# Attention kernel on one core: key norms as two split-format matmul passes, squares split by GpSimd, query norms issued first

## The reference, cut to what matters

```python
q, k, v = (cproj(Wq), cproj(Wk), cproj(Wv))      # complex, 16 heads of 64
qr = q * phase[None]; kr = k * phase[None]       # rotary
E = jnp.exp(jnp.clip(-mu[:, None, None] * dt[None], MIN_EXP, 0.0))
s = jnp.einsum('bihd,bjhd->bhij', qr, jnp.conj(kr)).real
qn = (q.real ** 2 + q.imag ** 2).sum(-1).transpose(0, 2, 1)
kn = (k.real ** 2 + k.imag ** 2).sum(-1).transpose(0, 2, 1)
maha = jnp.maximum(qn[..., None] + (E * E)[None] * kn[:, :, None, :] - 2.0 * E[None] * s, 0.0) / V[None]
logits = coef * jnp.log1p(maha / nu[None, :, None, None]) - 0.5 * DH_ * jnp.log(V)[None]
A = jax.nn.softmax(jnp.where(causal[None, None], logits, -jnp.inf), axis=-1)
out = jnp.einsum('bhij,bjhd->bihd', A.astype(v.dtype), v)
```

## Time and profile before

| what | us |
|---|---|
| median of 3 runs | 2018.23 |
| lowest and highest | 2016.56, 2019.1 |
| the profiled execution's own time | 2022.78 |
| its span in the profile | 2021.0 |

### The profile page before, as it was taken

The page is one execution under the profiler, slowest core; times in us unless marked ns, Lnnn a source line. Parts: engine busy times, 40 slices in busy tenths (PEclk is TensorE's granted clock), DMA queues, the critical chain, the costliest instruction groups (busy, mean ns, idle before and its releaser), DMA issues. The chain is left out here.

```text
span 2021.0 us, 32368 instructions
## 1 busy us (share of the span) xinstructions
PE 1818.7 (90%) x9824; PEld 1374.4 (68%) x9824; DVE 1603.8 (79%) x3302; ACT 1422.5 (70%) x2739; POOL 867.4 (43%) x686
## 2 busy tenths in 40 slices
PE   3777999689999999999999999999999997499998
PEld 2444666458777777777777777777777776266665
DVE  5589776678987987888888798798798886667776
ACT  3422444568988988888899898888888987444443
POOL 0299001055655655565565565566456553000000
PEclk9886999789999999999999999999999998699999
DMA  4000002322222222222222222222222221000000
GB/s 144 6 0 1 0 0 70 110 66 53 68 71 48 66 64 57 66 58 62 66 59 64 50 69 69 48 66 67 54 66 53 66 53 32 2 6 6 10 10 11
DMA packets 46341, 97.94 MB, mean 48 GB/s; under 512 B 6320, under 2 KB 20272, under 8 KB 46160
## 3 DMA queue, kind: packets, MB, share of 16 engines
q1 hardware_dynamic: 46160, 95.75, 18.9%
HBM read 18.13 MB, written 10.49 MB: 14 GB/s over the span
## 5 line engine op out<-in xcount | busy, mean ns | idle before, releaser
L1036 POOL TENSOR_TENSOR rot<-by_cos,crossed 128x1024 f32<-128x1024 f32 x128 | 305.3, 2385 | 507.4 <-PE pS L851 287.5
L1044 POOL TENSOR_TENSOR ek<-decay,knorm 128x128 f32<-128x128 f32 (+3 forms) x512 | 432.2, 877 | 38.1 <-ACT knorm L961 38.1
L1091 DVE CUSTOM_DVE_ANT_0 z<-u,lam,hp 128x128 f32<-128x128 f32 (+3 forms) x512 | 255.3, 555 | 117.2 <-ACT u L981 116.4
L953 ACT ACTIVATE z<-z,nmax 128x128 f32<-128x128 f32 (+3 forms) x512 | 281.4, 553 | 93.9 <-DVE nmax L1091 93.9
L851 PE MATMUL pS<-rot 128*128 128x128 f32 (+3 forms) x1024 | 302.8, 439 | 14.9 <-issue 14.6
L969 ACT ACTIVATE u<-u,qnorm 128x128 f32<-128x128 f32 (+3 forms) x512 | 246.2, 552 | 52.6 <-DVE u L1103 48.3
L1100 DVE SCALAR_TENSOR_TENSOR pS<-pS,ek 128x1280 f32<-128x1280 f32 x128 | 191.6, 1497 | 69.7 <-PE pS L851 69.7
L851 PEld LDWEIGHTS pS<-rot 128*128 128x128 f32 x1024 | 166.7, 193 | 113.5 <-issue 80.0
L886 PE MATMUL pS<-ident,z 128*128 128x128 f32 x1280 | 165.6, 277 | 40.6 <-DVE u L1103 33.6
L886 PEld LDWEIGHTS pS<-ident,z 128*128 128x128 f32 x1280 | 141.6, 142 | 84.0 <-ACT z L953 54.9
L1103 DVE TENSOR_TENSOR u<-pS,decay 128x1280 f32<-128x1280 f32 x128 | 190.9, 1492 | 4.4
(11 more groups left out here) (235 smaller groups left out, 3927.7 us busy)
## 6 DMA issues: line engine op xcount, KB each, us to landing
crossed<-by_sin SPq DMA_DIRECT2D x256, 256.0 KB, 3.6
trig_d<-reduced_f SPq DMA_DIRECT2D x16, 256.0 KB, 4.2
trig_d<-turns_f SPq DMA_DIRECT2D x16, 256.0 KB, 4.4
cos<-trig_d SPq DMA_DIRECT2D x16, 256.0 KB, 3.5
sin<-trig_d SPq DMA_DIRECT2D x16, 256.0 KB, 3.3
w_raw<-in_w SPq DMA_DIRECT2D x3, 704.0 KB, 7.8
x_sb<-in_x SPq DMA_DIRECT2D x4, 512.0 KB, 6.6
wqk_raw<-in_wqk SPq DMA_DIRECT2D x16, 128.0 KB, 3.0
```

The source lines that it names most:

```text
L953: last = a.activation(z[:, span(I)], z[:, span(I)], ACT.Exp, bias=nmax[:, I:I + 1], scale=-1.0, accum_out=rsum[:, r % 4, I:I + 1])
L1036: g.tensor_tensor(rot[:], by_cos[:], crossed[:], ALU.add).then_inc(S["rot_done"], 1)
L1044: last = g.tensor_tensor(ek[:, span(I)], decay[par][:, span(I)], knorm[:, 0:(I + 1) * P], ALU.mult)
L1091: last = v.tensor_tensor_reduce(z[:, span(I)], u[:, span(I)], lam[par][:, near(I)], hp[par][:, NEG_COEF:NEG_COEF + 1], HIGHEST, ALU.add, A ...
```

## The change

The key norms are now computed by two float32r matmuls of a float32r matrix of ones (`ones_r`) with a low half and a high half of the key squares. The halves are made by POOL: a cast of the key squares to float32r (`key_hi`) and a subtraction (`key_lo`), in a new piece `split(i, r+2)` at the end of POOL's step, ahead of the next step's `rotate`. On PE the query norms now come ahead of the key norms, and the key norms wait for the split. ACT's `square` waits for the previous split before it overwrites `squares`. ACT makes `ones_r` once at the start. `stats` shares the memory of `ek`.

```diff
@@ tensor
             def norms(i, r):
                 n = i * 16 + r
                 wait(pe, S["sq_done"], n + 1)
-                wait(pe, S["norm_done"], n)
                 wait(pe, S["qn_done"], n)
                 if live(i, r - 2) and parity(r - 2) == 0:
                     wait(pe, S["val_done"], values_made(i, r - 2))
-                pe.matmul(s.p6[:], s.ones[:], squares[:, N:2 * N], start=True, stop=True).then_inc(S["kn_done"], 1)
                 for I in range(TILES):
                     last = pe.matmul(s.p5[:, I:I + 1], squares[:, I * P:(I + 1) * P], s.ones[:, 0:1],
                                      start=True, stop=True)
                 last.then_inc(S["q2_done"], 1)
+                wait(pe, S["split_done"], n + 1)
+                wait(pe, S["norm_done"], n)
+                pe.matmul(s.p6[:], ones_r[:], key_lo[:], start=True, stop=False)
+                pe.matmul(s.p6[:], ones_r[:], key_hi[:], start=False, stop=True).then_inc(S["kn_done"], 1)
@@ scalar
                 wait(a, S["cos_done"], n + 1)
                 wait(a, S["q2_done"], n)
+                wait(a, S["split_done"], n)
                 a.activation(squares[:], s.pQK[:], ACT.Square).then_inc(S["sq_done"], 1)
...
+            a.activation(ones_r[:], s.ones[:], ACT.Copy).then_inc(S["ones_done"], 1)
@@ gpsimd
+            def split(i, r):
+                n = i * 16 + r
+                wait(g, S["sq_done"], n + 1)
+                wait(g, S["kn_done"], n)
+                apart(g, S["pool_passed"])
+                g.tensor_copy(key_hi[:], squares[:, N:2 * N]).then_inc(S["split_hi"], 1)
+                wait(g, S["split_hi"], n + 1)
+                g.tensor_tensor(key_lo[:], squares[:, N:2 * N], key_hi[:].bitcast(F32),
+                                ALU.subtract).then_inc(S["split_done"], 1)
+
             def a_step(i, r):
                 if live(i, r + 1):
                     rotate(i, r + 1)
                     spread(i, r + 1)
+                if live(i, r + 2):
+                    split(i, r + 2)
                 if building(LAM, i, r):
                     build(i, building(LAM, i, r))
```

More of the change, by code:

```diff
@@ L754, in attention_phase @@
         rot = sb("rot", [P, 2 * N])
+        key_hi = sb("key_hi", [P, N], F32R)
+        key_lo = sb("key_lo", [P, N], F32R)
+        ones_r = sb("ones_r", [P, P], F32R)
         knorm = sb("knorm", [P, N])
@@ L766, in attention_phase @@
         rinv = sb("rinv", [P, 4, TILES])
-        stats = sb("stats_at", [P, TT, 6])
+        stats = ek[:, 0:TT * 6].rearrange("p (t c) -> p t c", c=6)
         names = ("w_in trig_in0 trig_in1 w_hi w_lo hp_done arg_done decay_done decay2_done lnv_done lam0_done "
-                 "lam_done qk_done bs_done crossed_in cos_done sq_done rot_done norm_done q2_done qn_done kn_done "
+                 "lam_done qk_done bs_done crossed_in cos_done sq_done split_hi split_done ones_done rot_done norm_done q2_done qn_done kn_done "
                  "ek_done s_done w_done t_done relu_done ln_done zred_done exp_done v_done "
@@ L925, in a_step @@
                     weigh(i, r - 2)
+            pe.wait_ge(S["ones_done"], 1)
             steps(nc.tensor, a_step)
```

## The result

| | median us | lowest, highest |
|---|---|---|
| before, 4 runs | 2017.39 | 2013.72, 2019.1 |
| after, 4 runs | 2083.57 | 2078.27, 2086.41 |

Three of the runs of before are those of the first part; the fourth lowers its median from 2018.23. The ratio is 1.0328, 95% interval 1.0299 to 1.0356: the change costs 66 us. The profiled execution of after took 2078.27 us. The page of after, the lines that answer to the earlier trace rows and those of the peaks and of the split; then the waits of its attention stage, 410 to 1700 us (who waited for whom: total us, times, longest).

What follows compares the result with a forecast made beforehand. Bound by an ACT-DVE chain in odd steps and a loop through PE's scores in even ones. Collision +22, odd builds +15, even builds +2, loop turns -3, filling and `ones_r` +2: +38, giving 2056 us; range 2030 to 2165.

Steps and rivals of the forecast that it cites:

- rival C: DVE doesn't give way between peaks; split ends later, turn late by 0.7 (odd), 0.3 us (even): 2083 us; chance 0.13.
- No gain from PE: Key norms on PE: 0.4 us a pair saved, 51 us over 128 pairs, almost all going into existing waits.
- the two loops of the first part: Odd steps: chain through ACT and DVE, 9.46 us; even steps: distances, turn, values, weigh, scores, some 10.2 us.
- The cast: POOL's cast of the key squares to float32r: taken as 0.77 us, bounds 0.48 and 1.57.
- The collision in the ordinary odd step: Cast starts inside DVE's 512-column peak, last peak waits: +0.45 us in 50 odd steps without building, +22 us.
- The sign that the key norms wait for POOL in all steps: Profile sign on PE: key norms wait for POOL's split in every step, the turn for their followers in build steps alone.
- rival A: Cast wins against DVE's 512-column peak: +1.7 us in odd steps, 2165 us in all; chance 0.20.
- Build steps by PE's wait: Late split delays key norms, project and turn by 1.2 us: 14 odd build steps by 1.1, +15 us.
- Even steps: Peaks' +0.45 us costs nothing, 0.74 to spare; only 16 even build steps pay 0.15 each, +2 us.
- rival K: PE's longer waits lower its clock in the attention stage, granted clock below 0.95; over 2400 us; chance 0.04.
- The stall is hidden: Ordinary odd step: PE's turn, delayed by the split, still ends ahead of the clamps, by 0.3 us.
- Loop turns: Seven turns of the loop, where PE is late: 0.4 to 0.5 us saved at each, -3 us.

Runs made afterwards that it cites:

- e1: Kernel before with only PE's order changed: query norms ahead of the key norms, which stay one float32 matmul, no split; 2019.95 us, ratio 1.0002.
- e9: Changed kernel with project ahead of the norms, high half made by ACT, and three empty semaphore increments on POOL ahead of its subtraction; 2047.01 us.
- e4: Changed kernel with one more empty semaphore increment on DVE ahead of the peaks, which start 0.09 us later; 2142.82 us, ratio 1.0615.
- e6: Changed kernel plus thrown-away float32 key norms on PE ahead of its wait for the split, in odd-head steps only; 2066.17 us, ratio 1.0263.
- e7: Changed kernel with PE's project of the next pair moved ahead of both norms; 2061.39 us, ratio 1.0236.

## Why the prediction was right, and where its sizes were wrong

The direction and the collision came as forecast; after is 2083.6 against 2056, inside a range that is wide, 2030 to 2165. It is also the number of rival C, 2083. What speaks for the forecast's mechanism is not the time but the lines: the cast starts inside the 512-column peak, and the last peak takes 0.82 us. Of the rest, the path through the build steps was wrong, and two terms were missing.

- **No gain from PE.** Right. e1 shows that the order costs nothing and gives nothing. e9, in which neither the turn nor a peak of an ordinary odd step is held up, has 9.47 us there, not less: the 0.4 us that PE saves on a pair are nowhere to be seen, as the two loops of the first part said.
- **The cast.** The record's mean is 0.97 us, but that contains its wait; bare it is 0.61, against the 0.77 taken. The Trainium skill's page (GPSIMD Engine Reference, Engine selection) led to an estimate of 0.6, and the trace agrees with it (0.61). My choice was the higher row.
- **The collision in the ordinary odd step.** The order of events was right to 0.04 us, the size was 0.34 instead of 0.45 (the same working with a cast of 0.61 gives 0.29), and the count was wrong. I booked 50 steps. The profile has 4 in an odd head, some 30, because the front step and the one behind it, whose square is late as in a build step, aren't of this kind. So the term is about 10 us, not 22. The sign that the key norms wait for POOL in all steps was wrong: in even steps PE comes late enough to wait 0.14 us at most.
- **The front step, not seen.** This is the first term that was missing: +10.7 us. I took every odd step that doesn't build as one kind. I had written that "a tenth of a microsecond decides" about rival A, and did not ask which steps shift the peaks by a tenth. The Trainium skill (SBUF — State Buffer, Who interferes with whom) lets the order of requests decide who blocks; e4 (0.09 us, +59 us) and e9 (0.24 us, -62 us) show just that, and in the front step the rule gives the other result than in its neighbours.
- **Build steps by PE's wait.** Forecast 14 x 1.1 = 15. The second build step is 1.10 us longer in each of the seven heads, the first 0.87 in e6, where the clock holds: 13.7 together. The size was right, the path was not. The forecast had `project` delayed and the turn late by 1.2 us. The runs show ACT's `key_norms` waiting 0.73 us for the key norms ahead of the clamps, while the turn ends before the clamps do, and e7, with `project` first, leaves these steps as long. That the two paths give nearly the same number is luck.
- **Even steps.** Forecast +2, all of it in build steps; the row has +1.9, by luck. The first build step of the even heads takes 10.72 us in after and 10.80 in before, so it lost nothing, and the second is at the loop turn. The +1.9 comes from the first steps of the even heads, which are ordinary odd ones in length (9.47 to 9.80, once 11.02: +3.5), less 1.6 elsewhere.
- **The clock, rival K, given 4 in 100.** This is the second missing term, some 21 us by e6 against after. I had worked out K only for a clock that falls for good. What came was in between, 25 stretches of about 3.5 us and a granted clock of 0.97 over the stage, not below the 0.95 of its sign. The window view of before had shown such stretches only at loop turns, where PE also waits long, and I gave the new waits of 1.4 us no price of that kind. "The stall is hidden" held for the 1.36 us themselves, but not for what the clock did after them.
- **Loop turns.** Forecast -3, measured +6.9. This sum lies between 78.8 and 92.1 in the thirteen kernels, and what orders it is the clock: in their profiles the 46 turns with a stretch at 1.2 GHz take 14.85 us in the mean (13.64 to 16.64), the 32 without one 13.31 (12.58 to 14.44). Before has one in three of its six turns, after in all six, so, by an estimate from the two means, 3 x 1.54 = 4.6 of the 6.9 us go with it. That the change brings them is not shown: e1, without any split, has them in five of six (86.3 us) and costs nothing in the runs.

Taken together, the table's 62.2 us divide into 9.7 for ordinary steps (the even row in it), 10.7 front, 13.7 builds, 21.2 clock by e6, and 6.9 loop turns. This is the same table divided anew, with e6 as the divider, so that it adds up proves nothing. Without clock and loop turns it is 34, near the forecast's +38, but partly by luck, since the count of ordinary steps was too high by what the front steps took.

No version tried here beats the kernel before. By the two loops none should: what the split saves on PE isn't waited for, and what it adds on POOL is. That no order of these pieces could is not shown.

## What to carry to other kernels

Before moving work to GpSimd, lay its request times beside VectorE's instructions with two SBUF operands, for each kind of step apart, and look at who is first by less than 0.2 us. If the margin is that thin, the price is a range, and a few empty instructions can be worth more than a faster one. A wait on TensorE that other work hides is not free if it lets the clock fall: price it once with the clock held and once at 1.2 GHz for the work behind it. And when a result comes late, price every engine that reads it: here the key norms' own reader, ACT, was held up before the turn was.

## What was not expected of the hardware

- GpSimd's instructions and VectorE's peaks, which read two SBUF tiles, shut each other out for whole instructions (a peak of 0.48 us took 1.47), and even a VectorE copy of 128x10 was held up (0.46 us instead of 0.14). A blocked instruction's record contains the wait (0.61 became 1.15), so a mean duration in the profile is no price. The distances, which read one tile of PSUM and one of SBUF, kept their 1.49 us beside POOL.
- Which of them is first was settled by 0.04 us in e4 (1045.30 and 1045.34), and most steps went alike.
- TensorE's granted clock fell to 1.2 GHz for about 3.4 us after waits as short as 0.86 and 1.11 us in one step, or one of 1.37 us. Many waits of about 1.1 us in other steps passed without it, and so did 18 of the 26 of 1.36 or 1.37 us, the one ahead of 1017.11 among them; what sets them apart stays open. A thrown-away matmul in the wait kept the clock up in the profiled executions (25 stretches to 6 and 3).
